# A decoder layer on one NeuronCore: new prologue and tail, the down projection's contraction split 128 + 48, tokens renumbered

## The reference

```python
x = x + attn(layernorm(x))                # low-rank q/k/v, 16 heads, causal softmax over 128 keys
x = x + xattn(layernorm(x), ctx, ctx)     # 2 heads, decay mask instead of a softmax, group norm, gate
x = x + ffn(layernorm(x))

# ffn, 1024 tokens t, 16 experts e, inner width 176
logits = einsum('th,eh->te', x, gate_w)
topk_w, topk_idx = top_k(softmax(logits), 2)
h = swiglu(einsum('th,ehj->etj', x, w_gate_up), 176)
y = einsum('eti,eih,te->th', h, w_down, combine)     # combine: topk_w at topk_idx
y = y + swiglu(x @ shared_gate_up, 352) @ shared_down
```

## Time and profile before

| | us |
|---|---|
| median of 3 runs | 240.82 (240.66 to 242.6) |
| the profiled execution | 240.65 |
| its span, first to last instruction | 238.8 |
| PE busy | 226.9 (95% of the span) |
| DVE / ACT / POOL busy | 143.7 / 123.0 / 80.0 |

### The profile page before, as it was taken

One profiled execution on the slowest core, in us unless ns is written; L12 is line 12 of the kernel. 1 busy time (PEld: TensorE's weight loads), 2 busy tenths in 40 slices (PEclk: granted clock), 3 DMA queues, 4 the chain that ended last, 5 costly groups with the idle time before them and its releaser, 6 DMA issues.

```text
span 238.8 us, 5442 instructions
## 1 busy us (share of the span) xinstructions
PE 226.9 (95%) x1808; PEld 158.0 (66%) x1808; DVE 143.7 (60%) x442; ACT 123.0 (51%) x444; POOL 80.0 (33%) x95
## 2 busy tenths in 40 slices
PE   8977899999999999999999999999999999999992
PEld 6534567666676776889878878784555556556561
DVE  1568988979888778352989558976232322222181
ACT  2136998989898888924142620612333334333220
POOL 2221131111121101010375100266577777754152
PEclk9999999999999999999999999999999999999999
DMA  6999977600002800000601300013693333696683
GB/s 198 278 349 350 339 165 165 146 26 1 4 0 57 290 3 0 3 1 7 237 0 44 131 3 0 5 47 100 162 315 102 110 91 100 186 311 183 188 297 133
DMA packets 20638, 30.62 MB, mean 128 GB/s; under 512 B 2361, under 2 KB 15299, under 8 KB 20611
## 3 DMA queue, kind: packets, MB, share of 16 engines
q1 hardware_dynamic: 17603, 23.34, 32.7%
q0 software_dynamic: 2304, 6.29, 8.9%
q10 hardware_dynamic: 704, 0.64, 0.9%
HBM read 25.02 MB, written 5.24 MB: 127 GB/s over the span
## 4 chain that ended last, share of the span: by engine, by line
PE 75%; DVE 12%; DMA 3%; issue 2%; POOL 2%; ACT 2%; SPq 1%; DVEq 0%; ACTq 0%; POOLq 0%
PE bank L966 12%; PE bank L983 8%; PE bank L891 6%; PE bank L632 6%; PE bank L589 5%; PE bank L619 4%; PE bank L644 3%; PE bank L566 3%; PE bank L663 3%; PE bank L955 3%; PE bank L717 3%; PE bank L945 2%; DMA bxT<-in_wh_t 2%; PE bank L595 2%; PE bank L601 2%
## 5 line engine op out<-in xcount | busy, mean ns | idle before, releaser
L1100 ACT ACTIVATE pr_s<-bank,mx 128x128 f32<-128x128 f32 x128 | 45.4, 387 | 7.4 <-DVE mx L1336 7.4
L551 POOL DMA_INDIRECT expert_out<-by,prT x24 | 26.5, 1104 | 18.0 <-ACT by L1090 14.4
L1670 DVE COPY bxT<-bank 128x256 f32<-128x256 f32 x24 | 10.1, 423 | 37.2 <-PE bank L968 35.6
L966 PE MATMUL bank<-gu_s,bxT 128*64 x96 | 31.2, 466 | 0.0
L1090 ACT ACTIVATE prT<-bank 128x512 f32<-128x512 f32 (+1 forms) x56 | 27.5, 513 | 3.2 <-PE bank L644 2.0
L1100 ACT ACTIVATION_READ_ACCUMULATOR pr_s<-bank,mx 128x1 f32 x128 | 28.9, 226 | 0.0
L546 POOL DMA_INDIRECT qx_s<-ffn_in,prT x24 | 23.5, 978 | 14.3 <-issue 8.5
L1336 DVE TENSOR_REDUCE mx<-bank 128x4 f32<-128x512 f32 x32 | 21.2, 685 | 4.6 <-PE bank L619 4.6
L983 PE MATMUL bank<-dn_s,prT 88*64 x96 | 22.9, 379 | 0.4 <-ACT prT L1090 0.4
L891 PE MATMUL bank<-ck_s,sgu_s 128*128 128x256 f32 (+1 forms) x96 | 22.3, 382 | 0.0
L1255 ACT ACTIVATE pr_s<-bank 128x176 f32<-128x176 f32 x24 | 7.6, 318 | 27.1 <-PE bank L968 27.1
(11 more groups left out here) (206 smaller groups left out, 477.2 us busy)
## 6 DMA issues: line engine op xcount, KB each, us to landing
gu_s<-in_w_gu SPq DMA_DIRECT2D x8, 704.0 KB, 7.3
dn_s<-in_w_dn SPq DMA_DIRECT2D x4, 704.0 KB
early<-in_w_gu SPq DMA_DIRECT2D x8, 352.0 KB, 4.5
early<-in_w_dn SPq DMA_DIRECT2D x8, 176.0 KB
gu_s<-in_ctx_in SPq DMA_DIRECT2D x2, 512.0 KB, 9.6
ffn_in<-x_s SPq DMA_DIRECT2D x4, 256.0 KB, 2.5
cv_s<-expert_out SPq DMA_DIRECT2D x4, 256.0 KB, 3.3
x_s<-expert_out SPq DMA_DIRECT2D x4, 256.0 KB, 5.6
```

The costliest lines, as they stand in the source:

```text
L551: pool.indirect_dma_start(expert_out[:], bass.IndirectOffsetOnAxis(ap=idx[:, 1, k:k + 1], axis=0), by[:, k % RB, :], None).then_inc(dma_sc ...
L966: mm(bank[2 + i % 2][0:HT, 0:2 * I], bxT[:, i % 2, k, 0:HT], gu_s[:, k, bass.ds(e, 1), :], start=k == 0, stop=k == KD - 1, skip_group_chec ...
L1100: last = nc.scalar.activation(pr_s[:, n % 2, h, :], score_bank(n)[:, h * T:(h + 1) * T], ACT.Exp, bias=mx[:, n % 4, h:h + 1], accum_out=de ...
```

## The change

Five parts, in the order of the program.

1. Prologue: three matmuls of `keep_busy` between `weight_mean` and `wh_square`, two more after `ctx_keys(0, 1)`. The keys of tile 0 go into bank 7 and are copied by ACT (`act_first_keys`) while PE still projects the values; `qk_transpose(0)` waits for the keys' copy alone. `ctx_values(0, 0)` moves from the end of the attention to the place behind `qk_transpose(0)`.
2. Down projection: the contraction is 128 + 48. The 48 rows of an even block lie on partitions 0 to 47 and those of an odd block on 64 to 111, so that the rests of two blocks and two halves are four matmuls on four different quarters of the array. Because a matmul's operands share their partitions, SP now copies the rest of each lower half's weights (48 KB) into a free place of `dn_s`: 24 more DMAs; the staged down weights come in two DMAs instead of one. ACT copies the transposed hidden rows in two pieces.
3. The loop also computes `expert_up(21)`, and the tail's order is new: two whole pairs and the shared expert in four half pieces.
4. Tokens are numbered 8 p + t, so that partition p's rows of two tiles are 4 KB in one piece: four reads of 512 KB instead of eight of 256 KB, of which the third and fourth wait for the first and second.
5. DVE weighs tile 0 before it multiplies the last shared piece.

```diff
@@ numbering of the tokens, ffn_in
-    c[:, R_TOK:R_TOK + B] = T * np.arange(B)
-    c[:, R_TOK + B:R_TOK + 2 * B] = p + 1
+    c[:, R_TOK:R_TOK + B] = np.arange(B) + 1
+    c[:, R_TOK + B:R_TOK + 2 * B] = B * p
...
-                sp.dma_start(ffn_in[2 * q * T:2 * (q + 1) * T, :].rearrange("(b p) d -> p b d", b=2),
+                sp.dma_start(ffn_in.rearrange("(p b) d -> p b d", b=B)[:, 2 * q:2 * q + 2, :],
@@ SP
+            def stage_lower_rest(i, e):
+                if i >= E:
+                    sp.wait_ge(pe_expert_down, i - E + 1)
+                sp.dma_start(dn_s[rest_at(i), 1, (i ^ 1) % E, :],
+                             w_dn[bass.ds(e, 1), 128:I, :].rearrange("e p n -> p (e n)")).then_inc(dma_lower_rest[i // 2 % (E // 2)], 16)
+
+            for i in range(E):
+                stage_lower_rest(i, lower_expert(i))
...
+                else:
+                    for i in range(E, BLOCKS):
+                        stage_lower_rest(i, more_lower[i - E])
...
-            for t in range(B):
-                sp.dma_start(yg[t].rearrange("p k d -> p (k d)"),
-                             expert_out[0:SLOTS, :].rearrange("(b p k) d -> b p (k d)", k=2, b=B)[t]).then_inc(dma_token_outputs[t], 16)
+            for q in range(PAIRS):
+                if q >= 2:
+                    sp.wait_ge(dma_token_outputs[q - 2], 16)
+                sp.dma_start(yg_pairs[q], expert_out[0:SLOTS, :].rearrange("(p q n) d -> q p (n d)", q=PAIRS, n=4)[q]).then_inc(dma_token_outputs[q], 16)
@@ PE, prologue
             weight_mean()
+            keep_busy(bank[7], 3)
             wh_square()
...
             ctx_keys(0, 1)
+            keep_busy(bank[7], 2)
...
-            keys_values(0, 0)
-            keys_values(0, 1)
+            first_keys_values()
             qk_transpose(0)
+            ctx_values(0, 0)
@@ PE, experts
+            def expert_down_pair(i):
+                for b in (i, i + 1):
...
+                    mm(bank[4 + b % 2][0:HT, 0:D], bhT[:, b % 2, 0, 0:HT], dn_s[:, 0, bass.ds(e, 1), :],
+                       start=True, stop=False, skip_group_check=True)
+                    mm(bank[4 + b % 2][HT:T, 0:D], bhT[:, b % 2, 0, HT:T],
+                       dn_s[:, 0, b, :] if b < E else dn_x[:, (b - E) % SB, 0, :],
+                       start=True, stop=False, skip_group_check=True)
+                pe.wait_ge(dma_lower_rest[i // 2 % (E // 2)], 32 * (i // E + 1))
+                for b in (i, i + 1):
+                    mm(bank[4 + b % 2][0:HT, 0:D], bhT[rest_at(b), b % 2, 1, 0:HT], dn_s[rest_at(b), 1, (b ^ 1) % E, :],
+                       start=False, stop=True, skip_group_check=True)
+                for b in (i, i + 1):
+                    mm(bank[4 + b % 2][HT:T, 0:D], bhT[rest_at(b), b % 2, 1, HT:T],
+                       dn_s[rest_at(b), 1, b, :] if b < E else dn_x[rest_at(b), (b - E) % SB, 1, :],
+                       start=False, stop=True, skip_group_check=True).then_inc(pe_expert_down, 1)
@@ PE, tail (after the loop's last expert_down_pair(18))
             hidden_transpose(last - 3)
-            expert_up(last - 2)
-            expert_down(last - 3)
-            pe.wait_ge(dve_block_T, last)
-            shared_up(PAIRS - 1, 1)
             hidden_transpose(last - 2)
+            shared_up(PAIRS - 1, 1, (0,))
+            expert_down_pair(last - 3)
             expert_up(last - 1)
             expert_up(last)
-            expert_down(last - 2)
-            shared_up(PAIRS - 1, 2)
+            shared_up(PAIRS - 1, 1, (1,))
             hidden_transpose(last - 1)
             hidden_transpose(last)
-            expert_down(last - 1)
-            expert_down(last)
+            shared_up(PAIRS - 1, 2, (0,))
+            expert_down_pair(last - 1)
+            shared_up(PAIRS - 1, 2, (1,))
...
-                pe.wait_ge(dma_token_outputs[B - 2 + b], 16)
+                pe.wait_ge(dma_token_outputs[PAIRS - 1], 16)
@@ DVE, tail
-            shared_mul(PAIRS - 1, 2)
-            weigh_pair(0)
+            dve.wait_ge(dve_shared_added, PAIRS - 1)
+            weigh(0, 0)
+            weigh(0, 1)
+            shared_mul(PAIRS - 1, 2)
+            weigh(1, 0)
+            weigh(1, 1)
```

More of the change, by code:

```diff
@@ L316, in decoder_layer @@
         ctx_key_bank = lambda g, h: bank[6 if g else h]
-        ctx_value_bank = lambda g, j: bank[1 + j]
+        ctx_value_bank = lambda g, j: bank[1 if g and not j else 2]
+        first_key_bank = bank[7]
         rden_half = lambda b: bank[6 if b < B - 1 else 5][:, D:2 * D]
@@ L591, in keys_values, with first_keys_values @@
                     last.then_inc(pe_keys_values, 1)
+            def first_keys_values():
+                for k in range(2):
+                    last = mm(first_key_bank[:, 0:NOPE], ckvT[:, 0, k, :], wkv_s[:, k, 0:NOPE], start=k == 0, stop=k == 1)
+                last.then_inc(pe_first_keys, 1)
+                for k in range(2):
+                    last = mm(bank[3][:, NOPE:NOPE + D], ckvT[:, 0, k, :], wkv_s[:, k, NOPE:NOPE + D], start=k == 0, stop=k == 1)
+                last.then_inc(pe_keys_values, 1)
             def queries(b):
@@ L598, in qk_transpose @@
                 pe.wait_ge(dve_queries, b + 1)
[L599 removed]
+                pe.wait_ge(act_keys_values, b + 1) if b else pe.wait_ge(act_first_keys, 1)
                 for k in range(4):
@@ L811, in _ @@
             cross_transpose(B - 2)
-            ctx_values(0, 0)
+            ctx_values(0, 1)
             cross_scores(4)
             cross_scores(5)
-            ctx_values(0, 1)
             cross_scores(6)
@@ L953, in hidden_transpose @@
                     pe.wait_ge(dve_shared_added, PAIRS - 1)
-                for k in range(2):
-                    last = tr(hidden_bank(i)[0:IH, k * T:(k + 1) * T], bh[:, i % 2, k * IH:(k + 1) * IH], idf)
-                last.then_inc(pe_hidden_T, 1)
+                tr(hidden_bank(i)[:, 0:T], bh[:, i % 2, 0:128], idf)
+                tr(hidden_bank(i)[0:IR, T:2 * T], bh[:, i % 2, 128:I], idf).then_inc(pe_hidden_T, 1)
             def expert_up(i):
@@ L971, in expert_up @@
                 last.then_inc(pe_expert_up, 1)
[L973 to L987, removed]
-                last.then_inc(pe_expert_down, 1)
+            def expert_down_pair(i):
+                for b in (i, i + 1):
+                    e = expert(b)
+                    pe.wait_ge(act_hidden_T, b + 1)
+                    if b >= 2:
+                        pe.wait_ge(act_expert_out, b - 1)
+                    if b == 1:
+                        pe.wait_ge(dve_shared_hidden, SC * (PAIRS - 1) + 1)
+                    if b >= E:
+                        pe.wait_ge(dma_staged_down[(b - E) % SB], 32 * ((b - E) // SB + 1))
+                    mm(bank[4 + b % 2][0:HT, 0:D], bhT[:, b % 2, 0, 0:HT], dn_s[:, 0, bass.ds(e, 1), :],
[11 more added lines that the diff above has]
+                       start=False, stop=True, skip_group_check=True).then_inc(pe_expert_down, 1)
@@ L1055, in _ @@
                 expert_up(i)
-                if i + 4 < BLOCKS:
-                    expert_up(i + 1)
-                expert_down(i - 2)
-                expert_down(i - 1)
+                expert_up(i + 1)
+                expert_down_pair(i - 2)
                 read_expert(i + 2)
@@ L1104, in kv_out @@
             def kv_out(b):
+                if b == 0:
+                    act.wait_ge(pe_first_keys, 1)
+                    copy(qk[:, 0, D:D + NOPE], first_key_bank[:, 0:NOPE]).then_inc(act_first_keys, 1)
                 act.wait_ge(pe_keys_values, b + 1)
```

77 lines of the change are left out of this document (43 added, 34 removed).

## The result

The changed kernel takes 239.65 us (median of 8 runs, 239.19 to 240.15), the kernel before 240.74 beside it (8 runs): ratio 0.994, 95% interval 0.9911 to 0.9969. That is a gain of 1.1 us where 3.75 were forecast, and less than the 1% that can be told from no change. The profiled execution took 239.48 us with a span of 237.7 (240.65 and 238.8 before).

A forecast was written before the change was run, and what follows sets the result against it. PE was taken as the bound, with 75% of the chain. Gains of 0.6 + 0.85 + 3.1 + 0.4 = 4.95 less 1.2 given back to reads took 240.65 to 236.9 us, range 234.4 to 240.3.

The forecast's parts named there:

- The prologue: Start of the kernel: earlier copy of the keys shortens DVE's wait; net gain 0.6 us, between 0 and 0.9.
- the x load: Prologue: load of x tiles 2 to 7, thinly covered, is late next; price at most 0.2 us, within the 0.6.
- 0.4 of delay: Prologue: the three added matmuls ahead of `wh_square` were taken to delay PE by 0.4 us.
- `ctx_values(0, 0)`: Attention: moved off the path into PE's wait for DVE; gain 0.85 us, between 0.5 and 0.9.
- The down projection: Expert loop: rests on four array quarters side by side; 0.26 us a pair, 3.1 over twelve pairs, bounds 1.8 and 4.1.
- ACT's 0.39 us: Tail: PE's wait for ACT's copy of the hidden rows goes; counted as 0.4 us of gain.
- I take 8.4 us, the lower end: Tail: four chained reads, one always under way, take 8.4 us; PE waits 1.2 us for the fourth.
- N: Time mark in the tail: end of block 19's down projection, at 216.83 in the kernel before.
- The rival of chained reads: Tail: fourth read lands 11.3 us behind the first issue, PE waits 4.1, time 239.8; chance 0.15.
- The upper end: Top of the forecast range: chained reads with a prologue that gains nothing, 240.3 us.
- The rival of a POOL that bounds the loop: Expert loop: POOL's gathers and scatters, 5.12 us a pass, outlast PE's 4.99; time 237.8 or 238.5; chance 0.08.
- 4.95: Whole kernel: summed gains of 0.6 prologue, 0.85 `ctx_values`, 3.1 down projection and 0.4 tail wait, in us.

The follow-up runs named there:

- 9: Changed kernel without the chain of reads and with part 1 (prologue) undone: 237.50 us, ratio 0.9857 to the kernel before.
- 8: Changed kernel without the chain of reads and with part 2 undone (contraction 88 + 88, no rests copied by SP): 238.26 us, ratio 0.9882.
- 1: Changed kernel without the chain: third and fourth read no longer wait for the first and second; 235.9 us, ratio 0.9795 to the kernel before.
- 12: Changed kernel without the chain of reads and with the load of x tiles 2 to 7 in two: 236.02 us, ratio 0.9784.
- 6: Changed kernel with part 4 undone: old token numbering, eight unchained reads of 256 KB; 236.34 us, ratio 0.9804.
- run 10: Changed kernel, part 4 undone, eight unchained reads reordered (tiles 0, 1, 6, 7 first), shared product behind tile 1, PE's sums before tiles 4 and 5: 236.34 us.
- 3: Changed kernel plus sixteen small keep_busy matmuls between PE's shared part and its wait for the fourth read: 238.89 us, ratio 0.9894.
- 5: Kernel before, without the scatters of the empty blocks 22 and 23: 239.00 us against 240.93, ratio 0.9935.
- 11: As run 10 on the changed kernel, with the load of x tiles 2 to 7 also in two: 236.33 us, ratio 0.9803.

## Why the prediction was wrong

**Right, the prologue in part by luck.** The prologue: 0.6 forecast, 0.58 in the profile, with the x load next in line. But the 0.6 was 1.0 from DVE's wait less 0.4 of delay by the matmuls ahead of `wh_square`. The 1.0 came (DVE's copy of the keys starts at 16.87, before at 17.86); the delay did not (PE's queries start at 14.10 in both: `weight_mean`, whose passes had taken 0.60 us, took 0.32); and 0.4 went to the x load, which was priced at 0.2 at most. That load is late in some executions only: in the nine traces with the new prologue and the load in one piece, DVE waits 0 to 0.99 us for it, and the first row maximum starts 0.5 to 1.1 earlier than before. `ctx_values(0, 0)`: 0.85 forecast; the first `cross_mix` starts 1.25 earlier in all (111.39, before 112.64), so 0.67 for this. The down projection: 0.26 a pair forecast, 0.25 a pass measured, the rests in sets 0.27 apart, as the scores had said. ACT's 0.39 us went. Parts 1 and 2 alone were worth 1.2 to 1.6 (9) and 2.4 us (8) at the end. The change of layout cost 0.10 us ahead of the rests (169.44 - 169.13 - 0.21), as at 176.00; by the drain that the Trainium skill gives ("TensorE: Matmul & The Clock Gate", Part 2) it would be an estimated 0.05, and the measurement decides.

**Wrong: "I take 8.4 us, the lower end" for the four reads, "with one read always under way".** The term was in the sum, its size was off: 10.5 us, and a wait of 3.69, not 1.2. What stands around it came as forecast: with N at 215.02 the reads began at N + 6.26 (6.1 forecast), and PE was ready for the last rows at N + 13.24 (13.3). The 8.4 us are what four reads take without the chain (8.2 and 8.8). That the chain is the cause is shown by 1, 12 and 6. How it costs the 2.3 us is in part argued. One read under way did not fill the engines: while SP waits for a landing, issues, and the next read finds its way in, they run at 209 GB/s where run 1 had 379 in the same window. And the working counted 2.1 MB, the reads alone, where 3.08 MB moved until the fourth had landed: a read that is issued late has the stores of finished tiles beside it. At the 319 GB/s of run 1 the 3.08 MB would take an estimated 9.7 us, so the traffic would be some 1.5 us and the lower rate some 0.9. No run held the stores back to test this; run 10, whose unchained reads have stores in their midst, needs 9.8 us as well.

The rival of chained reads had a chance of 0.15, a wait of 4.1 and a time of 239.8. Its wait is near what came; that its time is too is luck, since it has neither the clock nor the end nor the gathers of the next paragraphs, which nearly cancel. (The upper end, 240.3, is 240.4 by its own terms.)

**Missing from the sum: the clock.** The prediction said that only PE's last eight records stand behind its wait, and left them the 1.89 us of rows 8. Behind 3.69 us of idling they took 3.01 (3 shows that it was the clock: 1.99 without the idling).

**Missing from the sum: the end.** The sum ended at DVE's last instruction, as the chain of waits does, and took the 4.17 us behind it as fixed. 1.88 of them were POOL's drain behind the scatters of blocks 22 and 23 (5). Their scatter moved from 229.49 and 233.64 to 225.34 and 226.72, because the changed tail ends both blocks 4.1 us sooner (ACT's copies at 224.68, before 228.83), and because the first of the two takes 1.07 us of POOL and not 3.85; why it took so long before is not shown. This gain hid most of the loss: with the old 4.17 us at its end the changed kernel's span would have been some 0.8 us longer than that of the kernel before.

**Missing from the sum: late gathers.** PE reached the first `expert_up` 1.16 us earlier (160.87, before 162.03) and the second pair's only 0.44 (166.06, before 166.50), so 0.72 went where it waits for gathered rows. The rival of a POOL that bounds the loop was nearer than its 0.08: from 177 to the last gather POOL never waits for longer than its usual 0.30, with 5.15 us of its own work against a pass of 5.00. The profiled execution lost nothing by it in the late passes, but in six of the eleven other traces of changed kernels one pass near 195 is 0.3 to 0.8 us longer, as in 11.

By the terms: 4.95 - 0.72 - 0.18 (`ctx_values`) = 4.05 of PE's 4.08; given back 3.75 and 1.11 where 1.2 were set; and 1.88 gained that stood in no term.

## What to carry to other kernels

A wait between transfers that share their engines must be paid by something. Before one accepts "one is always under way", count what else will be moving by then, and not only the transfers' own bytes: a transfer that is issued later shares the engines with all that started meanwhile. Where a wait is put on PE, what stands behind it may run at half clock, as here, so the price is the wait and the clock. And the end of a program is the last of all engines: read what each closes with (here a drain behind scatters of empty blocks), since a gain ahead of it may be hidden or doubled.

## What the runs showed of the hardware

- POOL's closing drain ended about 4 us behind its last scatter's issue span (233.64 + 0.97 to 238.6) in the kernel before, and 6.8 us behind it in the changed one, with reads and stores beside it (226.72 + 1.06 to 234.6; DMA share 0.98 and 0.96 from 227 to 231). What sets its length is not shown.
- The wait for gathered rows at the loop's start (0.2 to 0.7 us at about 165, and up to 0.25 between two blocks; in 3 the trace puts it down to DVE's copy of the rows) comes in seven of the fourteen traces. In those seven, and in no other, a DMA packet of the instruction queue of 16 KB lies between 162 and 163.5, beside the gather that PE then waits for. Window of the changed kernel, 162.5 to 163 (queue, kind: packets, MB, share):

```profile
q0 software_dynamic: 29, 0.10, 75.6%
q8 instruction: 1, 0.02, 12.0%
```

  That code loading delays the gather is a reading of this coincidence; no run moved the packet by itself, and it stays open.
- The clock fell behind 3.69 us of idling at the end in the changed kernel, and in one trace in the prologue behind waits of 0.81 and 0.94 us with little work between them (9; the kernel before has the same waits at 1.00). It stayed at 1.00 behind waits of 1.33 (1) and 1.86 us (12), and `keep_busy` matmuls held it in 3.
- Four float32 matmuls on four quarters of the array (48 rows x 64 columns) start within 0.02 us of each other, a set every 0.27 us, and the change of layout into them costs 0.10 us (169.44 to 169.71 above).
